# Second attention: a tile's tokens normalised and transposed one unit ahead

## The reference

```
x = x + tanh(g_xattn[0]) * xattn_8_heads (layernorm(x), ctx_768)
x = x + tanh(g_ffn[0])   * expert_choice (layernorm(x))
x = x + tanh(g_xattn[1]) * xattn_16_heads(layernorm(x), ctx_768)
x = x + tanh(g_ffn[1])   * routed_top2   (layernorm(x))

def xattn(x, context, Wq, Wk, Wv, Wo, bo):
    q, k, v = x @ Wq, context @ Wk, context @ Wv      # split into heads of 64
    attn = softmax(q k^T * 64 ** -0.5)
    return (attn @ v) @ Wo + bo
```

## Time and profile before

| | us |
|---|---|
| median of 3 runs | 2037.72 |
| lowest, highest | 2034.91, 2038.28 |
| the profiled execution, own time | 2034.79 |
| its span | 2033.0 |
| PE busy / DVE busy / ACT busy / POOL busy | 1857.0 / 1609.4 / 1560.9 / 646.6 |
| second attention in it, first to last transposed tokens | 1333.5 to 1885.1 |

### The profile page before, as it was taken

How to read it: one execution, slowest core, us unless ns; L and a number is a source line. 1 busy time by engine, 2 the same in 40 slices (tenths; PEclk the granted TensorE clock), 3 DMA queues, 4 the chain that set the end, 5 groups by cost and what they waited for, 6 DMA issues and landing times. The chain is left out here.

```text
span 2033.0 us, 73747 instructions
## 1 busy us (share of the span) xinstructions
PE 1857.0 (91%) x29130; PEld 1337.4 (66%) x29130; DVE 1609.4 (79%) x3619; ACT 1560.9 (77%) x2771; POOL 646.6 (32%) x893
## 2 busy tenths in 40 slices
PE   4999998883999999999999999968999999999698
PEld 3787886641666666666666667645666667777477
DVE  3889987796888888888888887767888888888544
ACT  3888987472998989898989898756777777888443
POOL 3687886311000000000000000034555555555465
PEclk8899999795999999999999999979999999999799
DMA  7544444392000000000000000046555554333233
GB/s 179 96 94 93 97 92 90 100 357 72 14 12 14 12 14 12 14 12 14 12 14 12 14 7 2 2 121 132 130 130 130 131 132 67 63 67 63 54 114 114
DMA packets 304575, 147.44 MB, mean 73 GB/s; under 512 B 235472, under 2 KB 289536, under 8 KB 304000
## 3 DMA queue, kind: packets, MB, share of 16 engines
q1 hardware_dynamic: 303824, 144.75, 29.1%
q10 hardware_dynamic: 560, 0.08, 0.0%
HBM read 55.45 MB, written 30.54 MB: 42 GB/s over the span
## 5 line engine op out<-in xcount | busy, mean ns | idle before, releaser
L1642 DVE TENSOR_TENSOR h<-g,h 128x1024 f16<-128x1024 f32 x256 | 313.2, 1223 | 140.8 <-ACT h L1587 140.8
L232 PEld LDWEIGHTS psE<-ew,h 128*128 128x128 f16 x6144 | 350.0, 98 | 54.5 <-issue 35.5
L232 PE MATMUL psE<-ew,h 128*128 128x128 f16 x6144 | 363.8, 219 | 11.8 <-DVE eo L1652 5.2
L232 PE MATMUL psH<-xg,ew 128*128 128x512 f16 x1536 | 355.9, 382 | 0.0
L1582 ACT ACTIVATE g<-psH,eb1T 128x512 f32<-128x512 f32 x512 | 330.3, 680 | 29.5 <-PE psH L232 23.0
L585 PE MATMUL psV<-Bw,cT 96*64 96x512 f16 x2304 | 320.5, 382 | 13.3 <-DVE vB L788 12.2
L683 ACT ACTIVATE vB<-psV 128x512 f16<-128x512 f32 x384 | 226.5, 590 | 107.1 <-PE psV L585 107.1
L762 POOL TENSOR_TENSOR E<-E,rden 128x512 f32<-128x512 f32 x192 | 200.1, 1042 | 331.6 <-DVE rden L797 331.5
L1587 ACT ACTIVATE h<-g 128x1024 f16<-128x1024 f32 x256 | 270.6, 1057 | 8.1
L1710 POOL MEMSET rbias<- 64x384 f32 x1 | 0.4, 411 | 855.2 <-POOLq L133 855.2
L232 PEld LDWEIGHTS psH<-xg,ew 128*128 128x128 f16 x1536 | 140.1, 98 | 184.2 <-issue 32.5
(11 more groups left out here) (256 smaller groups left out, 2792.0 us busy)
## 6 DMA issues: line engine op xcount, KB each, us to landing
keys_ahead<-ust SPq DMA_DIRECT2D x40, 512.0 KB, 4.7
u<-keys_ahead SPq DMA_DIRECT2D x40, 512.0 KB, 3.7
rawe<-in_L_ffn_w_dram SPq DMA_DIRECT2D x32, 256.0 KB, 3.1
wb<-rw SPq DMA_DIRECT2D x64, 128.0 KB, 2.0
rows<-places SPq DMA_DIRECT2D x110, 64.0 KB, 2.6
out_dram<-x SPq DMA_DIRECT2D x7, 512.0 KB, 3.2
context_T<-cT SPq DMA_DIRECT2D x64, 48.0 KB, 2.5
PT<-Ph SPq DMA_TRANSPOSE x192, 3.1
```

The costliest lines, as they stand in the source:

```text
L232: last = e.matmul(to, a, b, start=start and n == 0, stop=stop and n == 2, **flags)
L1642: e.tensor_tensor(h[:, 1 - par, 1, 2 * q:2 * q + 2, :], g32[:, 2 * q:2 * q + 2, :], h[:, 1 - par, 0, 2 * q:2 * q + 2, :], ALU.subtract)\
```

## The change

`nx` becomes `Unit(j, -1)` in both attentions for PE and ACT. So in the second attention the three token steps of tile t+1 stand in the odd (second) unit of tile t, and on PE behind values b. The pipelines of PE and ACT start one step earlier (-1) and end their loop at `U - 1`, with which the last 8 units are written out straight instead of in a loop. PE's `tokens` in the first attention waits on one more semaphore (`xt` besides `ct`).

```
--- before.py
+++ after.py
@@ -499,7 +499,7 @@
                 if first:
                     pipeline(eng, body, 0, last, lo, hi, 4)
                 else:
-                    pipeline(eng, body, 0, 2 * AHEAD, lo, 2 * AHEAD, RING * G)
+                    pipeline(eng, body, -1, 2 * AHEAD, lo, 2 * AHEAD, RING * G)
                     pipeline(eng, body, 2 * AHEAD, last, 2 * AHEAD + 4, hi, RING * G)

             with nc.Block() as block:
@@ -597,7 +597,7 @@
                                                         cT[:, a.ring, cl, :], start=n == 0, stop=n == 2)
                             last.then_inc(s[f"U{b}"], 1)

-                        nx = Unit(j, -1) if first else a
+                        nx = Unit(j, -1)

                         def ready():
                             if first and nx.on:
@@ -607,18 +607,17 @@
                         def tokens():
                             if nx.opens:
                                 wait(e, s["ln"], nx.t)
-                                wait(e, s["ct" if first else "xt"], nx.t - 1)
+                                wait(e, s["xt"], nx.t - 1)
+                                if first:
+                                    wait(e, s["ct"], nx.t - 1)
                                 for m in range(2):
                                     last = e.matmul(psX[half(m)], xn[:, nx.tp, half(m)], ident32[:], start=True,
                                                     stop=True)
                                 last.then_inc(s["X"], 1)

-                        if not first:
-                            tokens()
                         if a3.on:
                             values(a3, 1, "b")
-                        if first:
-                            tokens()
+                        tokens()
                         if a.on:
                             if a.opens:
                                 if first:
@@ -670,7 +669,7 @@
                         pipeline(e, body, -1, U + 4, 8, U - 1, 4)
                     else:
                         e.wait_ge(s["w"], 16 * 3)
-                        phases(e, body, U + 4, 8, U)
+                        phases(e, body, U + 4, 8, U - 1)

                 @block.scalar
                 def _(e):
@@ -732,7 +731,7 @@
                             pipeline(e, body, lo - 1, hi - 1 + 4 * (hi == U), max(lo - 1, 8), hi - 1, 4)
                     else:
                         e.wait_ge(s["nmr"], 1)
-                        phases(e, body, U + 3, 8, U)
+                        phases(e, body, U + 3, 8, U - 1)

                 @block.gpsimd
                 def _(e):
```

## The result

The changed kernel takes 2039.98 us (median of 18 runs, 2037.12 to 2042.61), the kernel before, run on the same chip, 2035.4 (18 runs, 2033.55 to 2039.52). The ratio is 1.002, 95% interval 1.0013 to 1.0027: slower by 4.6 us. 4.5 were predicted. (The time named was 2042.2, because the forecast started from a median of 3 runs of the kernel before, 2037.7; 18 runs have 2035.4.) How much of that agreement is right and how much is errors that cancel, the rest tells. Two executions of the experiments lie far outside, 10028.7 us in experiment 1 and 2391.29 us in experiment 3, the latter at a mean granted clock of 0.741; no ratio contains them.

The account below looks back on a forecast made before the run. The prediction took a round on DVE and ACT, not PE, to bound the second attention. Its terms, 3.1 + 1.1 + 0.3 + 0 = 4.5 us slower, added to 2037.7 gave 2042.2 us, range 2035 to 2050.

Parts of the forecast that it names:

- What bounds the kernel: Second attention: the pacing round closes on DVE and ACT, 8.36 us a tile below unit 80; the change takes nothing off.
- The first rival: Second attention: PE sets the pace, so removing the 0.36 us wait in 40 tiles saves 14.5 us: 2023; chance 0.10.
- The wait comes back: PE, second attention: the `xna` wait of 0.36 returns as a longer `value_lo` wait, about 0.5 a tile; gain 0.
- What it adds: ACT, second attention's odd step: exponential queued behind value copy b, starting 2.67 behind the scores instead of 2.57 or 2.66.
- The range's upper end: Whole kernel, 2050: the sum with 4 us for the semaphore and part of value copy b's missing overlap.
- Units below 80: Second attention, 40 tiles: the exponential's delay costs 3.0 us in 30 tiles and 0.1 in 10, together 3.1.
- Units 88 to 119: Second attention, still in a loop, 16 tiles: the exponential's delay in 12 of them costs 1.1 us.
- Units 80 to 87: Second attention, written out straight as before: 4 tiles x 0.09 = 0.4 us slower.
- Units 120 to 127: Second attention's end: at most 0.4 us of delay, while leaving the loop for straight code returns 0.5.
- The extra semaphore: PE, first attention's wait on `xt`: taken as 0; 1 us if paid in one unit in four, 4 us in all.
- nothing moves: Second attention: the delay of 0.1 is absorbed, leaving 2037.7, give or take 2; chance 0.17.
- Slower by much more: Second attention: value copy b costs its full length, the exponential 0.23 later still; 18.5 us slower, 2056; chance 0.08.

Follow-up runs that it names:

- experiment 1: Changed kernel without PE's extra wait on `xt` in the first attention; ratio to the kernel before 1.0014.
- experiment 3: Changed kernel with ACT's copy to `xTa` behind value copy b in the second attention; ratio to the kernel before 1.0017, and 1.001 when run again.
- experiment 4: Kernel before with a second token transposition on PE in each odd step of the second attention, behind values a; ratio 1.0169.
- experiment 5: Kernel before with a second token transposition on PE in each odd step of the second attention, only in units below 80; ratio 0.9989.
- experiment 7: Kernel before with one more reciprocal on DVE, and two waits, in the second attention's odd steps; ratio 1.0023.
- experiment 8: Changed kernel without the extra `xt` wait and with PE's transposition ahead of values b in the second attention; ratio to the kernel before 1.0001.
- experiment 2: Changed kernel with PE's transposition ahead of values b in the second attention, still one unit ahead; ratio to the kernel before 0.9998.
- experiment 6: Kernel before with a second token transposition on PE only from unit 80 on, in one step of eight; run once, 2037.97 us.

## Why the prediction was right, and where it wasn't

**What bounds the kernel: right, and shown.** The round closes on DVE and ACT, not on PE. Work added to PE below unit 80 costs nothing (experiments 4 and 5), 0.06 added to DVE costs 0.07 (experiment 7), and the removed `xna` wait gained nothing (experiment 8). The first rival, 2023, falls.

The Trainium skill (Perfetto Trace Analysis, Optimization Strategy) looks for gaps of the most contended engine and starts its inputs sooner. The prediction took PE for that engine, by its matmuls' busy time, and made 2023 the rule's forecast. That was a misreading: the same page (Identifying the Most-Contended Engine) doesn't judge TensorE by matmul busy time, but by its matmul work against the peak or by the share of weight loads. Weight loads were 31.45 of 50 us, DVE was busy 43.08. By weight loads DVE is the most contended engine below unit 80, and the runs agree: PE's inputs came sooner, its gaps grew from 3.0 to 4.6 of 50 us, and nothing was gained.

**The wait comes back: right in kind, too small in size.** I said about 0.5 a tile for `value_lo`; it is 0.79. The 0.5 was the room that the leaving transposition gives. The old wait of 0.36 for `xna` stood in front of the transposition and leaves too, so I should have added both: 0.36 + 0.44 = 0.80. This changes nothing in the time.

**What it adds: right in mechanism, too large by 0.03 of 0.10.** The exponential follows value copy b, by 0.47 (0.48 said), and stands at 2.64 behind the scores (2.67 said). The 2.67 was the sum of 0.91 in the second attention and 1.76 from the first; the second link is 1409.43 - 1407.70 = 1.73. Of a delay of 0.10, an error of 0.03 is a third. Experiments 2 and 3 show the cause from two sides. (The range's upper end has a slip: 2.67 + 0.23 is 2.90, not 2.85. The price of 13 to 15 us goes by the 0.23 and stands.)

**Term by term.** Units below 80: 3.1 predicted; the loop's 1.87 in 32 tiles is 0.058 a tile, for 40 tiles 2.3; the table's 1.87 + 1.08 = 2.95 contains units 10 to 12, which scatter by over 1 us, where the delay in all of unit 0 to 16 is about 0.5. Units 88 to 119: 1.1, measured 0.88. Units 80 to 87: 0.4, measured 0.35. Units 120 to 127: 0.4 of delay less 0.5 for the straight code, -0.1 together; measured -0.37. Experiments 2, 3 and 8 have -0.45 to -0.46 there without the delay, so the straight code returns the 0.5, and the delay costs only 0.08 in those four tiles where I had put 0.4 at most.

**The extra semaphore: wrong.** I took 0 because a steady unit hides it. I had named the unit in four that doesn't, with 1 us as its price, and then didn't count it. It is 0.9 (experiment 1). That the two prices meet is luck: I had 16 units at 0.06, the traces have six at 0.10 to 0.16.

**How much of the agreement is luck.** The terms of my sum, 4.5, measure 2.3 + 0.88 + 0.35 - 0.37 = 3.2. The rest of the stages' 4.8 is what I had at nothing: 0.95 for the wait in the first attention, about 0.3 in the first four units of the second beyond the delay (unexplained), and about 0.4 of scatter in units 10 to 12. So the delay was put too large, the wait was left out, scatter did the rest, and the sum came out. As the earlier trace rows showed the weights 0.32 late where the loop turns, the wait belonged in the sum: nothing covers an instruction that is itself what others wait for.

The other rivals: "nothing moves" is refused by the interval (1.0013 at its lower end) and by the stages. "Slower by much more" didn't come: value copy b overlaps its neighbours as in the first attention (0.18 and 0.47 between starts).

What stays open: the timed ratio of experiment 3, 1 to 1.7 thousandths, of which its trace explains about 1 us; and the 0.4 us in the first units of the second attention. Why timed ratios scatter by some 2 us where the loops agree to 0.2 can be placed, though not explained: from the last scores of the first attention to the first of the second, work that no edit touches, the twelve comparable traces take 997.90 to 1002.51 us.

## What to carry to other kernels

Before removing a wait from the busiest engine, follow one round and see whether that engine is in it; if the next wait on the same engine ends with another's work, the removed one only moves there. Where an engine works in the order of its code, a copy that waits for another engine shouldn't stand ahead of work that is ready sooner and has the pacing chain behind it: here that alone was 0.07 us per tile lost, and 2.5 us per launch gained where the same order had stood unnoticed. In a loop a met semaphore was free only where its instruction was early.

## What the runs showed of the hardware

A wait on a semaphore that has long been reached cost, in a loop, 0.10 to 0.16 us ahead of a late transposition on PE (experiment 1) and 0.09 us ahead of a maximum on DVE that waits for PE (experiment 7). It cost nothing where the engine still had work in front of it, nor ahead of the same maximum in straight code.

A loop whose body on PE has 720 matmuls stalls at each turn by some 8.5 us, other engines with it, and fetches 9 more instruction packets a turn; one with 714 does neither (experiments 4 and 6). PE's granted clock is partly at the lower level (0.80, 0.66) in the stretches with a stall. 8 matmuls too many cost 34 us, some forty times the 0.88 that the change under study moved in this loop.
